# Two-batch Mamba-2 mixer kernel: where the second batch's layer norm, transposes and dt product stand, and which engine prepares the softplus

## What is computed

```python
x = L0_attn_hidden_states                     # (2, 512, 512)
xn = _layernorm(x, axis=-1)
x = x + mamba2(xn, ...) + ffn(xn, ...)

# mamba2: proj = xn @ in_proj_w.T -> gate (8192), hBC (8192 + 2*1024), dt (128)
hBC = silu(conv4(hBC) + conv_b)               # depthwise, 4 taps
dt = softplus(dt + dt_bias)                   # 128 heads
A_cs = cumsum(-exp(A_log) * dt)               # in chunks of 128 tokens
# scan over 4 chunks of 128 tokens: Y_diag + Y_off + D * hs, then * silu(gate),
# RMS norm over each of 8 groups of 1024 channels, then @ out_proj_w.T
# ffn: xn @ W.T + b, plus xn @ A[:r].T @ B[:, :r].T for the rank r of (8, 16, 32, 64)
#      that softmax(xn @ gate_w.T + gate_b) favours
```

## Time and profile before

| | us |
|---|---|
| median of 3 runs | 1766.87 |
| lowest, highest | 1766.46, 1768.51 |
| the profiled execution | 1765.04 |
| its span in the trace | 1763.3 |
| busy: PE, DVE, ACT, POOL | 1666.0, 1354.8, 1187.2, 1084.6 |
| idle time of PE in the span | 97.3 |

### The profile page before, as it was taken

The page is one execution under the profiler, slowest core; times in us unless marked ns, Lnnn a source line. Parts: engine busy times, 40 slices in busy tenths (PEclk is TensorE's granted clock), DMA queues, the critical chain, the costliest instruction groups (busy, mean ns, idle before and its releaser), DMA issues.

```text
span 1763.3 us, 28877 instructions
## 1 busy us (share of the span) xinstructions
PE 1666.0 (94%) x9694; PEld 1368.8 (78%) x9694; DVE 1354.8 (77%) x2398; ACT 1187.2 (67%) x2436; POOL 1084.6 (62%) x1358
## 2 busy tenths in 40 slices
PE   5889999999999999999868899999999999999997
PEld 4677878787878888788656778787878787887875
DVE  4877787877778787877668677878787878778785
ACT  2357777777777777777414577777777777777773
POOL 4236667666766667666543267666766676667764
PEclk9999999999999999999979899999999999999998
DMA  4144344334433344333132343344434443344431
GB/s 144 36 126 126 130 138 138 121 123 136 138 127 124 129 138 138 120 127 120 34 105 61 116 138 128 114 138 138 134 119 127 138 138 125 118 137 138 135 105 47
DMA packets 82434, 212.03 MB, mean 120 GB/s; under 512 B 11056, under 2 KB 27696, under 8 KB 82032
## 3 DMA queue, kind: packets, MB, share of 16 engines
q1 hardware_dynamic: 82288, 210.20, 36.8%
HBM read 207.01 MB, written 3.15 MB: 119 GB/s over the span
## 4 chain that ended last, share of the span: by engine, by line
PE 72%; DVE 17%; ACT 5%; issue 4%; DMA 1%; POOL 0%; SPq 0%; DVEq 0%; POOLq 0%; ACTq 0%
PE bh L454 20%; PE bg L454 17%; PE bo L593 15%; PE by L569 6%; DVE cv L618 5%; PE bt L561 4%; PE bt L580 4%; PE bt L600 2%; DVE acc L636 2%; ACT cv L258 2%; DVE mt L827 1%; DVE S L643 1%; DVE by L819 1%; PE bo L540 1%; PE bt L454 1%
## 5 line engine op out<-in xcount | busy, mean ns | idle before, releaser
L391 POOL TENSOR_TENSOR wl<-raw,wh 128x256 fp32r<-128x256 f32 x576 | 527.6, 947 | 146.1 <-ACT wh L254 146.1
L438 POOL TENSOR_TENSOR wol<-raw_o,woh 128x256 fp32r<-128x256 f32 x256 | 184.6, 743 | 483.0 <-ACT woh L358 483.0
L618 DVE SCALAR_TENSOR_TENSOR cv<-bh,par_sb,cv 128x511 f32<-128x511 f32 (+2 forms) x408 | 304.6, 747 | 191.0 <-ACT cv L258 185.8
L267 ACT ACTIVATE mt<-cs_row,cs_tok 128x128 f32<-128x128 f32 x1024 | 324.4, 389 | 0.0
L593 PE MATMUL bo<-woh,xh 128*128 128x512 f32 x512 | 212.7, 415 | 2.8 <-POOL xl L426 2.8
L593 PE MATMUL bo<-woh,xl 128*128 128x512 f32 x512 | 201.7, 394 | 0.0
L593 PE MATMUL bo<-wol,xh 128*128 128x512 f32 x512 | 199.9, 390 | 0.0
L325 ACT ACTIVATE xh<-xg 128x512 fp32r<-128x512 f32 x128 | 81.0, 633 | 166.1 <-DVE xg L823 166.1
L263 ACT ACTIVATE bh<-cv 128x512 f32<-128x512 f32 x136 | 81.8, 601 | 160.5 <-DVE cv L618 160.5
L426 POOL TENSOR_TENSOR xl<-xg,xh 128x256 fp32r<-128x256 f32 x256 | 182.6, 734 | 9.9 <-ACT xh L325 9.9
L811 DVE SCALAR_TENSOR_TENSOR sg<-tg,bg 128x512 f32<-128x512 f32 x128 | 87.9, 687 | 124.9 <-ACT tg L354 124.9
(11 more groups left out here) (168 smaller groups left out, 3354.5 us busy)
## 6 DMA issues: line engine op xcount, KB each, us to landing
raw<-in_w_step SPq DMA_DIRECT2D x128, 512.0 KB, 3.6
cs_row<-cs_rows SPq DMA_DIRECT2D x128, 512.0 KB, 4.3
raw_o<-in_w_out SPq DMA_DIRECT2D x128, 256.0 KB, 2.7
ec_row<-ec_rows SPq DMA_DIRECT2D x256, 96.0 KB, 3.7
raw<-in_w_bc SPq DMA_DIRECT2D x16, 512.0 KB, 4.1
acc<-in_x SPq DMA_DIRECT2D x2, 1024.0 KB, 8.6
mt<-in_w_ffn SPq DMA_DIRECT2D x2, 1024.0 KB, 7.6
out_dram<-acc SPq DMA_DIRECT2D x2, 1024.0 KB, 4.9
```

Of the source, the lines that this page charges most:

```text
L267: e = act.activation(mt[:, m % 2, h, chunk(j)], cs_row[:, m % 2, h, chunk(j)], ACT.Relu, bias=cs_tok[:, b, j, 2 * m + h:2 * m + h + 1], sc ...
L391: e = pool.tensor_tensor(wl[:, n % 2, part], raw[:, n % 2, part], wh[:, n % 2, part].bitcast(F32), ALU.subtract)
L438: e = pool.tensor_tensor(wol[:, 1 - u, part], raw_o[:, 1 - u, part], woh[:, 1 - u, part].bitcast(F32), ALU.subtract)
L618: dve.scalar_tensor_tensor(out=cv[:, u, k:], in0=src[:, 0:L - k], scalar=par_sb[:, un % UNITS, TAPS - 1 - k:TAPS - k], in1=cv[:, u, k:], o ...
```

## The change

Five things are moved or rewritten. The layer norm statistics of batch 1 stand on DVE at the end of iteration 60 of batch 0, its normalised tokens at the end of iterations 61 and 62 (two of four token blocks each). Iteration 64 holds PE's transposes, into the banks `bh` and `bg` in turns instead of into `bo`, with ACT's and DVE's copies, and after step 62's output product the dt product of batch 1, now into `bh`; the ag product, now into `bg`, follows the last sum of squares. The dt and ag weights are one tile of 784 columns, which is the first tile of a batch in the ring `raw`/`wh`/`wl`; batch 1's first two tiles are loaded and split in iterations 62 and 63. ACT makes the maximum and the absolute value of dt straight from PSUM (Relu, Abs), and takes over the copies of ag and of `uT`. In each batch the feed-forward product stands behind the first B/C product; in batch 1 the last group's `ms` is placed inside the softplus series and its addition into `acc` behind the series. POOL's long subtractions and additions are cut into pieces of 256 columns. SP stores batch 0's output behind the second B/C tile's load.

```diff
@@ constants
-LOADS = GROUPS + STEPS
+LOADS = 1 + GROUPS + STEPS
@@ sync
-            for b in range(NB):
-                sp.wait_ge(p_wol, did(b * STEPS - 1))
-                sp.dma_start(raw_o[:, 0, :], w_dt).then_inc(ld_pw, 16)
-                sp.dma_start(raw_o[:, 1, 0:KT * AG], w_ag).then_inc(ld_pw, 16)
+            load(dtag(0))
+            for b in range(NB):
                 sp.wait_ge(t_d, did(b * STEPS - 1))
-                sp.dma_start(raw_f, w_ffn).then_inc(ld_pw, 16)
-                for g in range(GROUPS):
-                    load_pair(b * LOADS + g, w_bc[g])
-                    if b == 0 and g == 1:
-                        load_x(1)
+                sp.dma_start(raw_f, w_ffn).then_inc(ld_ffn, 16)
+                if b == 0:
+                    load(bc(0, 0))
+                load(bc(b, 1))
+                if b == 0:
+                    load_x(1)
+                else:
+                    store(b - 1)
+                for g in range(2, GROUPS):
+                    load(bc(b, g))
...
-                    if has(m + 2):
-                        load_pair(b * LOADS + GROUPS + m + 2, w_step[m + 2])
+                    if m + 2 < STEPS or b + 1 < NB:
+                        load(step(b, m + 2))
@@ scalar
+            def token_hi(b, j):
+                act.wait_ge(pe_, b * PRO_PE + j + 1)
+                act.activation(xTh[:, b, :, chunk(j)], bank_t[j % 2][:, :].rearrange("p (k t) -> p k t", k=KT),
+                               ACT.Copy).then_inc(pa, 1)
...
+                act.wait_ge(pe_, b * PRO_PE + PE_DT)
+                act.activation(dm, bh[:, :], ACT.Relu, bias=hp[:, 0:1])
+                act.activation(dab, bh[:, :], ACT.Abs, bias=hp[:, 0:1]).then_inc(pa, 1)
+                act.wait_ge(pa, b * PRO_ACT + ACT_ABS)
                 act.activation(de, dab, ACT.Exp, scale=-1.0).then_inc(pa, 1)
+                if b > 0:
+                    split_ffn(b)
+                act.wait_ge(pe_, b * PRO_PE + PE_AG)
+                act.activation(ag[:, :, :].rearrange("p j c -> p (j c)"), bg[:, 0:NJ * AG], ACT.Copy).then_inc(pa, 1)
+                split_hi(bc(b, 1))
...
+                act.wait_ge(pe_, b * PRO_PE + PE_UT)
+                act.activation(uT, by[0:MAXR, :], ACT.Copy).then_inc(pa, 1)
@@ gpsimd
+                    split_lo(dtag(0))
+                pool.wait_ge(a_ffn, b + 1)
+                for part in pieces(KT * HID):
+                    e = pool.tensor_tensor(wlf[b][:, part], raw_f[:, part], whf[b][:, part].bitcast(F32), ALU.subtract)
+                e.then_inc(p_ffn, 1)
+                if b == 0:
+                    split_lo(bc(0, 0))
+                pool.wait_ge(pv, b * PRO_DVE + PRO_DVE_XN)
+                for j in range(NJ):
+                    for part in pieces(HID):
+                        e = pool.tensor_tensor(acc[:, b, j, part], acc[:, b, j, part], b_row[:, part], ALU.add)
+                e.then_inc(pp, 1)
+                for g in range(1, GROUPS):
+                    split_lo(bc(b, g))
...
+                    if m == STEPS - 3 and b + 1 < NB:
+                        inverse_dev(b + 1)
@@ tensor
+            def turn_tokens(b, j):
+
+                pe.wait_ge(pv, b * PRO_DVE + (PRO_DVE_VAR + j + 1 if j < 2 else PRO_DVE_XN + j - 1))
+                for k in range(KT):
+                    mm = pe.transpose(bank_t[j % 2][:, chunk(k)], xn[:, j, chunk(k)], ident[:, :])
+                mm.then_inc(pe_, 1)
...
+            def project_ffn(b):
+                pe.wait_ge(p_ffn, b + 1)
                 pe.wait_ge(v_acc, did(b * GROUPS - 1, NJ))
...
+                    if m == STEPS and b + 1 < NB:
+                        pe.wait_ge(v_h2, did(un - 1))
+                        turn_tokens(b + 1, 0)
+                        pe.wait_ge(v_sg, did(n - 1))
+                        turn_tokens(b + 1, 1)
                     if has(m - 1):
...
+                    if m == STEPS and b + 1 < NB:
+                        turn_tokens(b + 1, 2)
+                        turn_tokens(b + 1, 3)
@@ vector
+            def soft_log(b):
...
+                if b > 0:
+                    mean_square(b * GROUPS - 1)
+                link(b, dve.tensor_scalar(dh, dw, SERIES[7], None, ALU.mult))
...
             for b in range(NB):
-                prologue(b)
...
+                soft_log(b)
+                if b > 0:
+                    add_group(b - 1, b * GROUPS - 1)
+                decays_and_route(b)
...
+                    if b + 1 < NB and m == STEPS - 4:
+                        norm_stats(b + 1)
+                    if b + 1 < NB and STEPS - 3 <= m < STEPS - 1:
+                        for j in range(2):
+                            norm(b + 1, 2 * (m - (STEPS - 3)) + j)
```

342 lines of the change are left out of this document (178 added, 164 removed).

## The result

The changed kernel takes **1745.53 us** (median of 4 runs, 1742.7 to 1747.96) against 1766.66 for the kernel before on the same chip: ratio 0.9878, 95% interval 0.9861 to 0.9895, so 21 us less. The forecast was 1750.4 with a range of 1741 to 1757. The profiled execution of the changed kernel is its slowest, 1747.96 us with a span of 1746.2; its forecast span was 1746.8.

The account below looks back on a forecast made before the run. PE bounds the kernel, with idle time worth taking only at the batch hand-over and the start. Gains of 14.7 us at the hand-over and 1.8 in batch 0 sum to 16.5: median 1750.4 us, range 1741 to 1757.

Parts of the forecast that it names:

- What bounds the kernel: Whole kernel: PE, busy 1666.0 of 1763.3 us; idle time worth asking for only at hand-over and start.
- Entry: Layer norm inserts in iterations 61 to 63: PE 2.8, then 4.6, then 6.3 us late; bounds 4.0 and 8.
- To the dt product: From line 561 of step 63 at 871.2 through dt product at 880.1; clock loss taken as nothing, bound 1.6.
- Series: Batch 1's softplus on DVE: instructions about 1.3 us instead of 0.69 beside POOL, +4.1 in all, ending at 897.2.
- The new wait before feed-forward: PE, ready at 896.3, waits 3.7 us for the `acc` addition at 900.0, plus 2.0 for slow clock; product ends 912.9.
- Router: DVE after the `acc` addition: beside POOL's remaining ten pieces it loses 6.0 us, so `um` is ready at 913.2.
- From `um` to the tap: Line 513 to batch 1's first tap: 2.2 us instead of 1.5, tap at 915.4 instead of 930.08.
- Batch 0: Start of kernel: ACT copies transposes earlier, `xTl` complete at 21.0 instead of 23.1; gain 1.8 us, bounds 0 and 4.
- Relu and Abs: New functions on ACT: no added table load, so no cost; a load in the chain would be about 1.3 us each.
- engines do not take turns: Rival at hand-over: DVE loses little to POOL, PE has no wait, tap at 907, total 1742; chance 0.2.
- The slower case: Rival: short waits keep PE's clock at 0.50 through some 35 us of work from 868.7 to 913, total 1781; chance 0.03.

Follow-up runs that it names:

- store-first kernel: Changed kernel, but SP again stores batch 0's output ahead of batch 1's feed-forward weight load; 1758.62 us, ratio 0.9966.
- one pass: Changed kernel with the adapter product of `xn` with `w_ag` in one pass of three, 32 of 48 matmuls left out per batch; 1742.55 us, ratio 0.9874.
- slots: Changed kernel with batch 1's layer norm put one instruction at a time into DVE's two waits per step, iterations 59 to 63; 1733.12 us, ratio 0.9823.
- bias early: Changed kernel with batch 1's bias additions moved into POOL's idle time in the last two steps; 1747.32 us, ratio 0.9896.
- late store: Kernel before the change with only the store of batch 0's output moved behind batch 1's second B/C load; 1766.67 us, ratio 1.0008.
- late start: Changed kernel with five spare statistics instructions (3.1 us) on DVE ahead of batch 0's layer norm; 1741.88 us, ratio 0.9870.
- long pieces: Changed kernel with POOL's low part of `w_ffn` in one 2048-column instruction and the bias in 512-column ones; 1751.75 us, ratio 0.9926.
- add early: Changed kernel with `ms` after the reciprocal, the `acc` addition after the series' first instruction, and POOL's bias held until `um`; 1745.03 us, ratio 0.9872.
- wide form: Adapter product as 12 matmuls of 512 columns plus 4 transposes, in two kernels combining several edits to the changed kernel; 1736.78 us (0.9833) and 1732.32 us (0.9818).

## Why the prediction was right, and where it was not

The forecast gave 14.7 us at the hand-over and 1.8 in batch 0. The trace shows 17.3 and nothing; the median, in all, 21. That the profiled execution's span of 1746.2 lies so near to its forecast of 1746.8 is luck: 2.6 us too little at the hand-over and 1.8 too much in batch 0 cancel.

- **What bounds the kernel:** right. PE's busy time stayed, the idle 24 us of the hand-over went to 1.3, and everything behind the first tap keeps its distance.
- **Entry:** right in sum, for partly wrong reasons. PE is 4.5, 5.6 and 6.9 us late against 2.8, 4.6 and 6.3. The wait for the statistics is 2.86, as forecast from the earlier trace rows; but it was followed by 3.8 us at a clock of 0.57 (835.27 took 1.98 instead of 1.09), which I had priced nowhere. The pairs of blocks took 1.84 us, not 2.4, so PE's next two waits for `xt` were 0.78 and 1.09 us, not 1.9 and 1.8, and PE lost 1.1 and 1.3 us more in the two steps, not 1.8 and 1.7. Statistics were not hit by POOL: 2.46 us in both kernels, though POOL works beside them now. By the Trainium skill (SBUF — State Buffer, "Who interferes with whom") a DVE instruction with at most one input in SBUF, outside the two-port modes, doesn't contend with GpSimd; the 2.46 agrees.
- **To the dt product:** 877.83 to 880.55 (where the next product starts) against 880.1, and DE is ready at 882.7 against 882.1. The gap of 1.28 us did not bring the clock down.
- **Series:** the mechanism was right, the size too large. Its instructions beside POOL's 256-column pieces took 0.99 us each and the last 1.10, against 1.3 forecast and 0.69 alone: DVE loses 0.3 to 0.4 us each time, not a whole piece of 0.6. The store-first kernel is the control: POOL idles there, and the six take 4.32 us:

```profile
883.34 4.32 DVE L765 SCALAR_TENSOR_TENSOR tg<-tg,sg 128x512 f32<-128x512 f32 x6
```

POOL loses as well: its eight pieces took 8.28 us there in the changed kernel. The addition ended at 898.3 instead of 900.0.

- **The new wait before feed-forward:** it is not in the profiled execution, where I had 3.7 us and 2.0 for the slow clock behind it. The failed term is the adapter product: 8.6 us for 5.3 (B/C, 7.2 for 5.5 + 1.8, held), so PE came at 899.87 instead of 896.3. The runs show the wait itself to be real: as soon as PE has less to do (one pass), it stands there with 5.35 us and slow matmuls behind it. With the clock up through most of the adapter product alone (slots, 5.95 us for it) it is 0.18 us; the 1.86 of bias early goes with the addition that came 2.1 us later. Wait or slow clock, the end is nearly the same: `um` at 83.8 or 82.8 us after step 60.
- **Router:** ready at 909.6 against 913.2, of which 1.7 came from the series and the rest from its own size: 11.3 us from the addition's end, not 13.2. PE and DVE do arrive nearly together, as forecast.
- **From `um` to the tap:** 2.0 us against 2.2. The tap came 2.6 us before its forecast, all of it from the series, the router and the missing wait.
- **Batch 0:** 2.95 us at its first tap against 1.8, inside the bounds of 0 and 4. Its fate is the clock's: all of it went in the long form of the stretch before step 1, and of the five traces with this batch 0 four reach step 1 earlier than the kernel before did (139.43), by 0.5 to 4.9 us. The kernel before scatters as well: with the late store, which leaves its batch 0 as it was, it reached step 1 at 142.61.
- **Relu and Abs:** no added table load; ACT's three instructions lie from 880.75 to 882.68 without a gap. The Trainium skill (ScalarE: Activation LUTs, "Table sets: the hidden batching unit") puts both functions in every set, and this trace agrees.

Of the rivals, "engines do not take turns" is refuted as a mechanism (7.81 for 2.29 us; 11.45 for 4.32), though its time of 1742 lies nearer to the median than the forecast does: the turns were real and their size lay between its and mine. The slower case did not come; the longest stretch at the lower clock in the hand-over was 11 us.

Left open: what decides whether the clock falls in the narrow adapter product. In batch 1 it fell after 16 of its 48 matmuls in the changed kernel and about there in store first and late start, only in the last eight in four others with the same matmuls (slots, long pieces, bias early, add early), and in the wide form not at all. Open too is what decides between the two forms of the stretch before step 1.

## What to carry to other kernels

A bound hand-over is a bundle of chains. Here four ended within some 4 us of each other (DVE's series and addition, PE's products, the router, POOL's splits), so taking 7 us from one bought nothing. Look up what comes next behind each before cutting any.
When work must go into a full pipeline, put it one instruction at a time where the engine already waits; in one piece of 2.5 us it delays everybody.
When an instruction is made to wait, list its whole queue: the bias could wait, the split behind it could not.
Before two traces are compared by their ends, find a stretch of like work whose length changes with the clock, and compare ahead of it.

## What the runs showed of the hardware

- DVE and POOL hold each other up in some instructions: four normalising instructions of 2.29 us took 7.81 beside POOL instructions of 0.9 to 4.7 us, while the four statistics instructions took 2.46 with and without POOL beside them. The length of POOL's pieces sets the price: six series instructions took 4.32 us with POOL idle, 5.96 beside pieces of 1 us, 11.45 beside pieces of 5.05 and 1.7.
- The clock fell to its lower level behind waits of 2.9 us (0.57 for 3.8 us), 4.05 (0.69 for 9.8) and 5.35 (2.04 us for four matmuls that take 1.07 at the full clock), and without a wait in matmuls of 68 columns (0.53 for 11 us). It did not fall behind waits of 0.8 to 1.3 us. In between it went either way: a wait of 1.92 us was followed by four matmuls in 1.38 us, one of 1.86 by the same in 1.17.
- One and the same stretch of 91 matmuls behind the wait of 4.05 us takes 21.1 to 21.4 us (clock 0.92 to 0.93) or 23.9 to 24.3 (0.80 to 0.82), in all 28 cases of 14 traces. With what the clock does before it, the same instructions of batch 0 reach step 1 between 134.50 and 139.43 us. A difference of 3 us between two single traces of this kernel means nothing unless the place is named.
